# The last pass of three graph sums, in two parts: the last full chunk's tail between them, short mixes, halves

## The chip, the cores and the metric

The kernel runs on one core of one Trainium2 chip. The metric is device time in microseconds of one execution. A core has TensorE (PE, matmuls; PEld its weight loads), VectorE (DVE), ScalarE (ACT), GpSimd (POOL, which here issues the row gathers) and SyncE (SP, which issues plain DMAs).

## The reference

A graph of N = 12500 nodes with 128 features and 212500 edges, sorted by destination. Two relational layers, then one plain layer, each with a sum over the edges that end in a node:

```python
def rgcn(x, W, SW, b):                    # twice, 8 relations
    xt = einsum('nd,rde->rne', x, W)
    agg = segment_sum(xt[rel, src], dst)
    return relu(agg + x @ SW + b)
x1 = rgcn(x, w1, sl1, b1)
z  = layernorm(x + rgcn(x1, w2, sl2, b2))
feat = relu(z @ W1 + b1)                  # second part
h   = feat * d_invsqrt                    # d_invsqrt = max(degree, 1) ** -0.5
agg = segment_sum(h[src], dst)
out = layernorm(z + (feat - agg * d_invsqrt) @ W2 + b2)
```

## The kernel before

**Tiles, groups, passes.** The edges are cut into tiles of 128, seven tiles (KG) make a group, two groups a pair (PAIR), eight groups (RING) an iteration. There are 1661 tiles, thus 29 full iterations (IT) and six groups left over: five of seven tiles and one of two (`LEFT`). The kernel makes three passes over all edges: `relational_sum` twice and `plain_sum` once, each a block of its own with all engines meeting between them. Each pass gathers a 128-feature row per edge from a table in HBM: the input, then x1, then h. A pass needs the whole table of the one before it.

**A relational pass.** GpSimd (`Gathers.run`, L530) issues one indirect DMA per tile (L538) into a ring of 56 tiles. It is held by `idx_ready` alone, which ScalarE raises when it copies the indices of a pair whose ring slots have been summed. TensorE zeroes a PSUM bank (L666), in pass 1 also counts the edges per node (L675, added up by VectorE at L762), and sums a group with one matmul per tile (L681) against a one-hot matrix that VectorE made (L715, L718 for the counts, L720). It waits for all tiles of the group first (`wait_rows`, L566). ScalarE copies the bank out (L628). At the end of an iteration TensorE mixes all its groups over the eight relations (L689, eight matmuls; a float32 matmul leaves two records) and VectorE adds each group's 64 columns to the accumulator (L772). The offsets of a pair's tiles come from the table `off_i`, seven integers per group, which TensorE loads into registers.

**The plain pass.** No relations, no mix: TensorE sums a pair into one bank (L845) and VectorE adds it (L888).

**Chunks and tails.** The nodes are cut into 25 chunks (NCH) of 512, the last of 212 (two blocks of 128 where others have four). `by_chunk` (L458) is the order of every engine: for each chunk the iterations that its nodes still need, then `late`, the chunk's dense tail. In pass 1 that is the self-loop matmul's result plus the sum (L1089), activation (L1066), transposes (L971), copy (L1094) and store. Pass 2 adds a residual, a layer norm (L1392, L1396, L1194, L1403), the matmul with W1 (L1177), L1260, L1202, L1265 and three stores. In pass 3: L1338, L971, L1362, L1365, L978, L1341, L1328, L1369, a layer norm (L1373 to L1403) and the store of the output. Semaphores order the engines; each engine's own order is as written. For the last two chunks `by_chunk` runs the remaining iterations, then the six left-over groups as one iteration, then the tails of both chunks step by step together:

```python
    reach(NCH - 1)
    iteration(IT, LEFT)
    late(eng, two, [])
```

The prologue computes how many rounds a pass needs (`rounds_i`): one, unless some tile or group spans more nodes than a window has, or the left-over groups reach below the last two chunks (L360, L361).

## Time and profile before

| | us |
|---|---|
| median of 3 runs (6350.53 to 6352.94) | 6351.35 |
| the profiled execution | 6353.09 |
| its span, first to last instruction | 6351.3 |
| GpSimd busy | 4719.5 (74%) |
| TensorE busy | 3434.3 (54%) |
| VectorE busy | 1586.1 (25%) |
| ScalarE busy | 507.8 (8%) |
| mean granted TensorE clock, share of full speed | 0.645 |

Busy leaves out time in which an engine issues, waits or runs control instructions. An engine with 74% may thus be the one that never rests. The span falls into pass 1 (until about 2135), pass 2 (until 4253) and pass 3.

### The profile page before, as it was taken

What the parts mean: (1) busy time and instruction counts of PE and PEld (TensorE: products, weight loads), DVE (VectorE), ACT (ScalarE), POOL (GpSimd) and SP (SyncE); (2) the same over time, 40 slices, a digit from 0 to 9 for tenths busy, and PEclk for the clock granted to TensorE, in tenths of its full rate; (3) what the DMA queues carried; (4) which work ended last, traced back from release to release, by engine and by line L of the source; (5) the groups of instructions that cost most, each with busy time, mean ns of one, the idle gap of its engine ahead of it and who ended that gap; (6) DMA issues with size and microseconds to landing.
All of it is one profiled execution on the core that took longest, in us unless ns stands there. A gap on an engine that the chain in (4) does not pass through costs nothing. (4 is left out here: it accounts for less than half of the span.)

```text
span 6351.3 us, 51898 instructions
## 1 busy us (share of the span) xinstructions
PE 3434.3 (54%) x13350; PEld 2426.7 (38%) x13500; DVE 1586.1 (25%) x2504; ACT 507.8 (8%) x1112; POOL 4719.5 (74%) x4994
## 2 busy tenths in 40 slices
PE   4565556556565756566556656653444434344443
PEld 2333333333343534333333333333333334333333
DVE  4333433433343112122221212211111111111111
ACT  1000000000010101011110111110000000000000
POOL 6777777777777677777777777757777777777776
PEclk7776777767777767677667777765555555555555
DMA  3222222222222122222222222222222222222221
GB/s 74 59 59 59 59 56 59 59 59 59 59 59 59 52 64 74 61 69 69 69 69 61 77 61 69 69 60 58 63 61 64 62 57 68 58 62 62 62 63 55
DMA packets 207369, 396.37 MB, mean 62 GB/s; under 512 B 87746, under 2 KB 96756, under 8 KB 207332
## 3 DMA queue, kind: packets, MB, share of 16 engines
q0 software_dynamic: 159456, 326.88, 19.7%
q1 hardware_dynamic: 47876, 69.05, 3.4%
q8 instruction: 17, 0.28, 0.0%
q14 instruction: 20, 0.16, 0.0%
HBM read 363.49 MB, written 32.10 MB: 62 GB/s over the span
## 5 line engine op out<-in xcount | busy, mean ns | idle before, releaser
L538 POOL DMA_INDIRECT r_rows<-h_d,r_idx x1661 | 1568.8, 944 | 542.1 <-issue 505.9
L538 POOL DMA_INDIRECT r_rows<-x_d,r_idx x1661 | 1576.0, 949 | 531.5 <-issue 505.8
L538 POOL DMA_INDIRECT r_rows<-in_x_dram,r_idx x1661 | 1571.8, 946 | 533.7 <-issue 505.8
L681 PE MATMUL bank<-r_S,r_rows 128*128 128x128 f32 x6644 | 1218.9, 356 | 987.4 <-DMA r_rows<-in_x_dram,r_idx 455.9
L681 PEld LDWEIGHTS bank<-r_S,r_rows 128*128 128x128 f32 x6644 | 1135.5, 263 | 967.1 <-issue 957.2
L845 PE MATMUL bank<-r_S,r_rows 128*128 128x64 f32 x3322 | 768.4, 424 | 1111.2 <-DMA r_rows<-h_d,r_idx 1099.1
L845 PEld LDWEIGHTS bank<-r_S,r_rows 128*128 128x128 f32 x3322 | 726.4, 330 | 1155.7 <-DMA r_rows<-h_d,r_idx 621.2
L720 DVE TENSOR_TENSOR r_S<-bank,key 128x1792 f32<-128x1792 f32 x238 | 480.1, 2017 | 996.4 <-PE bank L681 993.7
L628 ACT COPY r_agg<-bank 128x512 f32<-128x512 f32 x476 | 279.1, 586 | 2558.2 <-PE bank L681 2558.2
L689 PE MATMUL bank<-r_agg,w1s 128*128 128x512 f32 (+1 forms) x480 | 446.7, 1099 | 24.1 <-ACT r_agg L628 24.1
L689 PE MATMUL bank<-r_agg,w2s 128*128 128x512 f32 (+1 forms) x480 | 446.3, 1098 | 24.1 <-ACT r_agg L628 24.1
L888 DVE TENSOR_TENSOR acc<-acc,bank 128x64 f32 x238 | 52.7, 222 | 1594.6 <-PE bank L845 1578.9
L715 DVE TENSOR_TENSOR r_hot<-bank,b_spot 128x1344 bf16<-128x1344 f32 x119 | 185.3, 1557 | 647.0 <-PE bank L681 641.6
L772 DVE TENSOR_TENSOR acc<-acc,bank 128x64 f32 x476 | 105.5, 222 | 794.8 <-PE bank L689 740.2
L718 DVE TENSOR_REDUCE r_part<-r_hot 128x192 bf16<-128x1344 bf16 x119 | 288.7, 2426 | 4.1
L689 PEld LDWEIGHTS bank<-r_agg,w1s 128*128 128x128 f32 x480 | 110.6, 237 | 315.1 <-issue 315.1
L689 PEld LDWEIGHTS bank<-r_agg,w2s 128*128 128x128 f32 x480 | 110.8, 237 | 314.4 <-issue 314.4
L666 PEld LDWEIGHTS bank<-zeros_bf 128*128 128x128 bf16 x476 | 53.3, 112 | 446.1 <-issue 293.3
L666 PE MATMUL bank<-zeros_bf 128*128 128x512 bf16 x327 | 152.7, 467 | 127.0 <-ACT r_agg L628 71.9
L523 ACT COPY r_idx<-src_i 128x14 int32 x360 | 73.1, 205 | 1728.0 <-PE bank L845 1728.0
L861 DVE TENSOR_TENSOR r_S<-bank,key 128x896 f32<-128x896 f32 x119 | 129.7, 1091 | 36.2 <-DVE acc L888 36.0
L675 PE MATMUL bank<-one_bf,r_part 128*32 128x1 bf16 x714 | 36.5, 166 | 156.4 <-issue 97.3
(142 smaller groups left out, 1300.8 us busy)
## 6 DMA issues: line engine op xcount, KB each, us to landing
r_rows<-in_x_dram,r_idx POOLq DMA_INDIRECT x1661, 2.5
r_rows<-x_d,r_idx POOLq DMA_INDIRECT x1661, 2.5
r_rows<-h_d,r_idx POOLq DMA_INDIRECT x1661, 2.5
d_xr<-in_x_dram SPq DMA_DIRECT2D x48, 256.0 KB, 2.7
x_d<-d_yr SPq DMA_DIRECT2D x24, 256.0 KB, 2.1
d_x1r<-x_d SPq DMA_DIRECT2D x24, 256.0 KB, 2.7
z_d<-d_zr SPq DMA_DIRECT2D x24, 256.0 KB, 2.3
feat_d<-d_fr SPq DMA_DIRECT2D x24, 256.0 KB, 2.1
```

The source lines that it names most:

```text
L523: act.copy(self.cols(p), self.c.src_i[:, bass.ds(i * UN + p * PT, PT)]).then_inc(self.idx_ready, 1)
L538: pool.indirect_dma_start(out=self.rows[:, s, :], out_offset=None, in_=self.table[:, :], in_offset=bass.IndirectOffsetOnAxis(ap=self.idx[: ...
L628: act.copy(agg[:, h, :, :], agg_ps[h % BUFS][:, :].rearrange("p (n r) -> p n r", r=NREL)).then_inc(agg_out, 1)
L666: pe.matmul(agg_ps[j][:, :], c.zeros_bf[:, :], c.zeros, start=True, stop=False, skip_group_check=True)
L681: mm = pe.matmul(agg_ps[j][:, bass.ds(offs[j * KG + k], TK)], g.rows[:, h * KG + k, :], S[:, pb, j * KG + k, :], start=False, stop=(k == t ...
L689: mm = pe.matmul(mix_ps[:, 0:groups * GN], W[:, r, :], agg[:, 0:groups, :, r], start=(r == 0), stop=(r == NREL - 1))
L715: ch.then(dve.tensor_tensor(hot[:, b, :, :], spots.unsqueeze(1).broadcast_to([P, PT, SPOTS]), bc_last(c.blocks.spot[:, at], SPOTS), ALU.is ...
L718: dve.tensor_reduce(part[:, b, :, :], hot[:, b, :, :].rearrange("p (j k) n -> p j n k", k=KG), AX.X, ALU.add)
L720: dve.tensor_tensor(S[:, b, :, :], c.iota[:, :].unsqueeze(1).broadcast_to([P, PT, TK]), bc_last(c.key[:, at], TK), ALU.is_equal).then_inc( ...
L772: ins = dve.tensor_tensor(window, window, mix_ps[:, j * GN:(j + 1) * GN], ALU.add)
L845: mm = pe.matmul(sum_ps[b][:, j * GN:(j + 1) * GN], g.rows[:, h * KG + k, :], S[:, b, j * KG + k, :], start=(k == 0), stop=(k == tiles[h] ...
L861: dve.tensor_tensor(S[:, p % BUFS, :, :], c.iota[:, 0:GN].unsqueeze(1).broadcast_to([P, PT, GN]), bc_last(c.key[:, bass.ds(i * UN + p * PT ...
```

## The change

- `by_chunk`: the six left-over groups become two parts, pair 0 (two groups) and pairs 1 and 2 (four groups). On every engine but GpSimd and SP the order is now: part one, tail of chunk 23, part two, tail of chunk 24. GpSimd's gathers keep their order.
- Within these parts TensorE mixes each pair by itself right after its sums (128 columns), and VectorE adds it right then. Full iterations mix all eight groups as before.
- The last pair (groups 4 and 5) waits for its gathers in two halves each: the first half of a group's tiles on the group's semaphore, the rest on one of two new semaphores.
- `off_i` gets 16 integers per pair in place of 14, set to zero in the prologue, and TensorE loads 16.
- The prologue's condition for a further round is tested per part. SP stores the last two chunks one after the other instead of stage by stage.

The diff, cut to its core (`...` marks what is left out):

```diff
+class Part:
+    def __init__(self, at, tiles):
+        self.at, self.tiles, self.groups = at, tiles, len(tiles)
+        self.pairs = range(at, at + len(tiles) // PAIR)
+    def of(self, h):
+        return self.tiles[h - self.at * PAIR]
+FULL = Part(0, [KG] * RING)
+LEFT = Part(0, [min(KG, TILES - g * KG) for g in range(IT * RING, NG)])
+LEFT_PARTS = [Part(0, LEFT.tiles[:PAIR]), Part(1, LEFT.tiles[PAIR:])]
+ENDS = len(LEFT.pairs)
...
+        c.off_i = sb("off_i", [1, NGP, OFFS], I32)
...
+        for at, part in enumerate(LEFT_PARTS):
+            first = IT * RING + part.at * PAIR
+            ch.then(dve.tensor_reduce(sp[:, 6 + at:7 + at], c.glo[0:1, first:first + part.groups], AX.X, ALU.min))
+            ch.then(dve.tensor_scalar(sp[:, 6 + at:7 + at], sp[:, 6 + at:7 + at], float((NCH - 2 + at) * CH), None,
+                                      ALU.is_lt))
+        ch.then(dve.tensor_tensor(sp[:, 6:7], sp[:, 6:7], sp[:, 7:8], ALU.max))
...
-    iteration(IT, LEFT)
-    late(eng, two, [])
+    for part, chunk in zip(LEFT_PARTS, two):
+        iteration(IT, part)
+        late(eng, [chunk], [])
...
+def halves(part, h):
+    tiles = part.of(h)
+    return (tiles + 1) // 2 if part is not FULL and h >= (ENDS - 1) * PAIR else tiles
...
+                    for k in range(part.of(h)):
+                        s, slot = h * KG + k, h if k < halves(part, h) else RING + h % PAIR
                         pool.indirect_dma_start(
                             out=self.rows[:, s, :], out_offset=None, in_=self.table[:, :],
                             in_offset=bass.IndirectOffsetOnAxis(ap=self.idx[:, s:s + 1], axis=0)
-                        ).then_inc(self.landed[h], 16)
+                        ).then_inc(self.landed[slot], 16)
...
+        tiles, half = part.of(h), halves(part, h)
+        if k == 0:
+            pe.wait_ge(self.landed[h], (i * KG + half) * 16)
+        elif k == half:
+            pe.wait_ge(self.landed[RING + h % PAIR], (tiles - half) * 16)
...
+                def mix(at, h0, groups):
+                    pe.wait_ge(agg_out, n + (h0 + groups + BUFS))
+                    pe.wait_ge(added, q * NIT + i + (at + 1))
+                    for r in range(NREL):
+                        mm = pe.matmul(mix_ps[:, 0:groups * GN], W[:, r, :], agg[:, h0:h0 + groups, :, r],
+                                       start=(r == 0), stop=(r == NREL - 1))
+                    mm.then_inc(mixed, 1)
...
-                        c.off_i[0:1, bass.ds(i * RING + p * PAIR, PAIR), :], engines=bass.OrderedEngineSet([pe.engine]),
+                        c.off_i[0:1, bass.ds(i * PR + p, 1), :], engines=bass.OrderedEngineSet([pe.engine]),
...
+                    if part is not FULL:
+                        mix(p, p * PAIR, PAIR)
+                if part is FULL:
+                    mix(0, 0, RING)
...
+                def add(at, starts):
+                    dve.wait_ge(mixed, q * NIT + i + (at + 2))
+                    for j, start in enumerate(starts):
+                        window = c.acc[:, bass.ds(start, GN)]
+                        ins = dve.tensor_tensor(window, window, mix_ps[:, j * GN:(j + 1) * GN], ALU.add)
+                        if j < len(starts) - 1:
+                            ch.then(ins)
+                    ins.then_inc(added, 1)
+                    dve.wait_ge(added, q * NIT + i + (at + 2))
...
+                    if ahead(part, p):
                         one_hot((p + BUFS) % PR, q, i + (p + BUFS) // PR, ch)
-                starts = load(c.gs_i, NPAD)
-                dve.wait_ge(mixed, q * NIT + i + 2)
-                for j, start in enumerate(starts):
-                    window = c.acc[:, bass.ds(start, GN)]
-                    ins = dve.tensor_tensor(window, window, mix_ps[:, j * GN:(j + 1) * GN], ALU.add)
-                    if j < len(starts) - 1:
-                        ch.then(ins)
-                ins.then_inc(added, 1)
-                dve.wait_ge(added, q * NIT + i + 2)
+                    if part is not FULL:
+                        add(p, starts[first:first + PAIR])
+                if part is FULL:
+                    add(0, load(c.gs_i, NPAD))
...
-        store(*two)
+        for ch in two:
+            store(ch)
```

## Rows read from the trace of the kernel before

**Rows 1.** costliest groups by line over the whole span; columns: line, engine, operation, tiles, shapes, count | busy us, mean ns of one | idle us before, by releaser

```profile
L538 POOL DMA_INDIRECT r_rows<-x_d,r_idx x1661 | 1576.0, 949 | 531.5 <-issue 505.8 <-ACT r_idx L517 25.7
...
L538 POOL DMA_INDIRECT r_rows<-h_d,r_idx x1661 | 1568.8, 944 | 542.1 <-issue 505.9 <-ACT r_idx L517 36.3
```

**Rows 2.** timeline, end of pass 1; columns: start us, us, engine, line, operation, tiles, count [idle before <-releaser]

```profile
2069.09 15.05 PE L689 MATMUL bank<-r_agg,w1s 128*128 128x512 f32 x16 [0.81 <-ACT r_agg L628]
...
2089.36 0.39 PE L666 MATMUL bank<-zeros_bf 128*128 128x512 bf16 x1 [1.23 <-ACT r_agg L628]
...
2094.17 2.01 DVE L720 TENSOR_TENSOR r_S<-bank,key 128x1792 f32<-128x1792 f32 x1
...
2099.86 3.35 PE L681 MATMUL bank<-r_S,r_rows 128*128 128x128 f32 x14 [5.33 <-DMA r_rows<-in_x_dram,r_idx]
...
2108.65 3.35 PE L681 MATMUL bank<-r_S,r_rows 128*128 128x128 f32 x14 [4.76 <-DMA r_rows<-in_x_dram,r_idx]
...
2114.03 11.39 PE L689 MATMUL bank<-r_agg,w1s 128*128 128x384 f32 x16 [0.75 <-ACT r_agg L628]
...
2125.56 1.98 DVE L772 TENSOR_TENSOR acc<-acc,bank 128x64 f32 x6 [21.11 <-PE bank L689]
...
2130.44 1.02 DVE L1094 COPY d_yr<-bank 128x512 f32<-128x512 f32 x2 [1.65 <-PE bank L971]
```

**Rows 3.** windows, one stretch; columns: us, PE, PEld, DVE, ACT, POOL busy, granted clock, DMA share

```profile
2091.00:2099.00 8.00, 3.35 (x14) 3.09 (x15) 5.35 (x5) 0.59 (x1) 6.16 (x7) 0.50 0.22 55
```

**Rows 4.** timeline, a tail inside the loop of pass 2

```profile
4124.43 0.69 DVE L1240 TENSOR_TENSOR d_pre<-bank,acc 128x512 f32<-128x512 f32 x1 [0.56 <-DVE acc L772]
...
4133.07 2.08 PE L1177 MATMUL bank<-gw1s,d_zT 128*128 128x128 f32 x8 [0.68 <-ACT d_zT L1198]
...
4136.67 0.69 DVE L1265 TENSOR_TENSOR d_hr<-d_fr,dinv 128x512 f32<-128x512 f32 x1 [0.79 <-ACT d_fr L1202]
...
4142.26 3.26 PE L681 MATMUL bank<-r_S,r_rows 128*128 128x128 f32 x14 [4.18 <-issue]
...
4148.73 1.82 PE L681 MATMUL bank<-r_S,r_rows 128*128 128x128 f32 x14
```

**Rows 5.** timeline, end of pass 2

```profile
4194.99 0.59 ACT L628 COPY r_agg<-bank 128x512 f32<-128x512 f32 x1 [1.19 <-PE bank L681]
...
4221.40 11.28 PE L689 MATMUL bank<-r_agg,w2s 128*128 128x384 f32 x16 [0.75 <-ACT r_agg L628]
...
4232.82 1.99 DVE L772 TENSOR_TENSOR acc<-acc,bank 128x64 f32 x6 [34.32 <-PE bank L689]
...
4248.11 1.03 DVE L1265 TENSOR_TENSOR d_hr<-d_fr,dinv 128x512 f32<-128x512 f32 x2
```

**Rows 6.** groups by line and shape, the two-block chunk's instructions

```profile
L1066 ACT ACTIVATE d_xT<-d_xT,b1s 128x256 f32<-128x256 f32 x1 | 0.5, 493 | 0.0
...
L1362 DVE TENSOR_TENSOR d_ag<-bank,dinv 128x256 f32<-128x256 f32 x1 | 0.4, 417 | 0.0
```

**Rows 7.** timeline of pass 3: a tail inside its loop, then its end

```profile
6216.72 0.57 DVE L888 TENSOR_TENSOR acc<-acc,bank 128x64 f32 x2 [15.53 <-PE bank L845]
...
6223.39 2.08 PE L1328 MATMUL bank<-gw2s,d_uT 128*128 128x128 f32 x8 [0.67 <-ACT d_uT L1341]
...
6228.99 1.11 DVE L1403 TENSOR_SCALAR d_o<-d_r,d_mv,d_rstd 128x128 f32<-128x128 f32 x4
...
6304.00 0.58 DVE L888 TENSOR_TENSOR acc<-acc,bank 128x64 f32 x2 [15.16 <-PE bank L845]
...
6326.80 0.94 POOL L538 DMA_INDIRECT r_rows<-h_d,r_idx  x1 [0.30 <-issue]
...
6326.88 4.38 PE L845 MATMUL bank<-r_S,r_rows 128*128 128x64 f32 x18 [5.55 <-DMA r_rows<-h_d,r_idx]
...
6331.39 0.57 DVE L888 TENSOR_TENSOR acc<-acc,bank 128x64 f32 x2 [9.35 <-PE bank L845]
...
6346.12 0.75 DVE L1403 TENSOR_SCALAR d_o<-d_r,d_mv,d_rstd 128x128 f32<-128x128 f32 x2
```

More of the change, by code:

```diff
@@ L34 @@
 TILES = -(-E // P)
[L35 to L36 removed]
+class Part:
[8 more added lines that the diff above has]
+ENDS = len(LEFT.pairs)
 NGP = NG // PAIR
[L38 to L39 removed]
+OFFS = 16
+assert NT % KG == 0 and min(LEFT.tiles) > 0 and NG % PAIR == 0 and RING % PAIR == 0 and PR % BUFS == 0
+assert LEFT.groups % PAIR == 0 and BUFS < ENDS < PR and PAIR == BUFS and PT <= OFFS
 CH = 512
@@ L203, in __init__ @@
         self.raw_in = [sem(f"raw_in{n}") for n in range(3)]
-    CONSTS = 11
+    CONSTS = 12
     BANKS = -(-NTB // 4)
@@ L530, in run, with iteration @@
     def run(self, pool, ready):
-        def iteration(q, i, tiles):
-            for p in range(len(tiles) // PAIR):
+        def iteration(q, i, part):
+            for p in part.pairs:
                 pool.wait_ge(self.idx_ready, (q * (IT + 1) + i) * PR + p + 1)
@@ L590, in relational_sum @@
     hot = sb("hot", [P, BUFS, PT, SPOTS], BF16) if counts else None
-    part = sb("part", [P, BUFS, PAIR, SPOTS], BF16) if counts else None
+    placed = sb("placed", [P, BUFS, PAIR, SPOTS], BF16) if counts else None
     hot_ready = sem("hot_ready")
@@ L621, in _, with iteration @@
         with act.Fori(0, rounds) as q:
-            def iteration(i, tiles):
+            def iteration(i, part):
                 n = act.snap(q * NG + i * RING)
@@ L625, in iteration @@
                 gate(act, c.passed)
-                for h in range(len(tiles)):
+                for h in range(part.at * PAIR, part.at * PAIR + part.groups):
                     act.wait_ge(summed, n + (h + 1 + RING))
@@ L629, in iteration @@
                              ).then_inc(agg_out, 1)
-                    if tiles is FULL and h % PAIR == PAIR - 1:
+                    if part is FULL and h % PAIR == PAIR - 1:
                         g.take(act, h // PAIR, q, i + 1)
@@ L724, in _, with ahead, part_steps @@
         first_steps = BUFS if counts else 0
-        def pass_steps(tiles):
-            pairs = len(tiles) // PAIR
-            ahead = pairs if tiles is FULL else max(pairs - BUFS, 0)
-            return (pairs + ahead if counts else 0) + len(tiles) - 1
-        round_steps = first_steps + IT * pass_steps(FULL) + pass_steps(LEFT)
+        def ahead(part, p):
+            return part is FULL or p + BUFS < ENDS
+        def part_steps(part):
+            adds = part.groups - 1 if part is FULL else len(part.pairs) * (PAIR - 1)
+            return (len(part.pairs) + sum(ahead(part, p) for p in part.pairs) if counts else 0) + adds
+        left_steps = [part_steps(part) for part in LEFT_PARTS]
+        round_steps = first_steps + IT * part_steps(FULL) + sum(left_steps)
         with dve.Fori(0, rounds) as q:
@@ L742, in _, with iteration @@
             gate(dve, c.passed)
-            def iteration(i, tiles):
-                n = dve.snap(q * NG + i * RING)
+            def iteration(i, part):
                 np = dve.snap(q * NGP + i * PR)
-                pairs = len(tiles) // PAIR
-                ch = Chain(dve, steps, q * round_steps + (i * pass_steps(FULL) + first_steps))
+                before = left_steps[0] if part is LEFT_PARTS[1] else 0
+                ch = Chain(dve, steps, q * round_steps + (i * part_steps(FULL) + (first_steps + before)))
                 def load(table, most):
                     _, values = nc.values_load_multi_w_load_instructions(
-                        table[0:1, bass.ds(i * RING, len(tiles))], engines=bass.OrderedEngineSet([dve.engine]),
+                        table[0:1, bass.ds(i * RING + part.at * PAIR, part.groups)],
+                        engines=bass.OrderedEngineSet([dve.engine]),
                         min_val=0, max_val=most, skip_runtime_bounds_check_because="clamped on the chip")
                     return values
+                def add(at, starts):
[7 more added lines that the diff above has]
+                    dve.wait_ge(added, q * NIT + i + (at + 2))
                 blocks_at = load(c.blocks.gb_i, DEG_COLS) if counts else None
-                for p in range(pairs):
+                starts = load(c.gs_i, NPAD) if part is not FULL else None
+                for p in part.pairs:
+                    first = (p - part.at) * PAIR
                     if counts:
@@ L814, in _, with iteration @@
         with act.Fori(0, rounds) as q:
-            def iteration(i, tiles):
-                if tiles is FULL:
+            def iteration(i, part):
+                if part is FULL:
                     for p in range(PR):
@@ L833, in _, with iteration @@
             gate(pe, c.passed)
-            def iteration(i, tiles):
+            def iteration(i, part):
                 np = pe.snap(q * NGP + i * PR)
-                for p in range(len(tiles) // PAIR):
+                for p in part.pairs:
                     b = p % BUFS
```

74 lines of the change are left out of this document (31 added, 43 removed).

## The prediction

> **What bounds the kernel now.** I first read the groups by line. GpSimd issues 1661 row gathers in each of three passes: 944 to 949 ns of work each and 0.30 us of issue idle, so one starts every 1.25 us [rows 1]. Its only other long idle time is at a seam: 25.7 us before pass 2's first gather, 36.3 us before pass 3's. Three passes at 1.25 us are 6.23 ms of the 6.35 ms span, so inside a pass TensorE, VectorE and ScalarE are covered. What the change can move is the stretch from the last gather of a pass to the next first gather, and from the last gather of all (start 6326.80) to the end [rows 7].
>
> The timelines show what fills them. In pass 1 the last sums are followed by one mix over six groups (384 columns) that starts at 2114.03 and takes 11.39 us, six adds that end at 2127.54, and the tails of chunks 23 and 24 together, whose last copy ends at 2131.46 [rows 2]. Pass 2 has the same from 4221.40, adds until 4234.81, and a longer tail until 4249.14 [rows 5]. Pass 3 has no mix: the last adds end at 6331.96, the tail at 6346.87 [rows 7], the span at 6351.3.
>
> **What the change does, part by part.**
>
> *Price of a short mix.* Sixteen records at 512 columns take 15.05 us, at 384 columns 11.39, so 128 columns are worth 3.66 us and a mix of one pair (128 columns) costs 11.39 - 7.32 = 4.1 us [rows 2]. The first add starts 11.5 us after the start of the long mix, so 4.2 after a short one. The Trainium skill, "Perfetto Trace Analysis", Matmuls, says that larger matmuls are more efficient than smaller ones when possible, which speaks against three mixes for one. By that rule the three would cost more than the 11.39 us. The rows give 12.3 against 11.4, nearly straight in the columns, so I add 0.9 us in all, most of it off the end.
>
> *TensorE, pass 1.* Pair 0 is summed before 2089. Its mix is over by 2093, but VectorE makes the one-hots for pair 2 first, until 2096.2 [rows 2]. Then two adds (0.6), the tail of chunk 23: first add 0.7, activation 0.7, four transposes 1.1, gaps: TensorE is free at about 2099.8. It used to sum group 2 long before and group 3 at 2099.86. Now it loads its offsets (a gap of 1.23 us before the zeroing matmul at 2089.36 [rows 2]) and counts: group 2 starts at 2101.3. A group takes 3.35 us with granted clock 0.50, the 1.2 GHz level [rows 2, 3], and 1.82 us at the higher level, 2.4 GHz; in pass 2 sums go from 3.26 to 1.82 us once TensorE has stayed at work [rows 4]. I take 3.35 for group 2, 2.6 for group 3 and 1.8 for group 4. Group 2 ends at 2104.7, group 3 at 2107.5, the mix of pair 1 runs 2108.3 to 2112.2 (0.8 us for the last copy, as before 2114.03). Group 4's rows had landed at 2108.65 [rows 2], group 5's two, two gathers later, at 2111.2: neither is waited for, so halves are worth nothing here. Group 4 ends at 2114.4, group 5 at 2115.2, mix 2116.0, adds 2120.2 to 2120.8. Before: 2127.54. Gain 6.7 us.
>
> *Tail of the short chunk alone, pass 1.* Before: 3.92 us from adds to last copy. Now 0.23 + add 0.42, activation 0.49 [rows 6], two transposes 0.6 (four 0.26 us records, by the rate of the eight in 2.08 [rows 4]), copy 0.42, gaps 0.15: 2.3. Gain 1.6. Pass 1 together 8.3.
>
> *Pass 2.* Pair 0's last copy is at 4194.99, so its mix starts at 4195.8, the adds at 4199.9 (VectorE makes one one-hot only and is not late), chunk 23's first instruction at 4200.7. In the loop the tail keeps TensorE until the end of L1177, 4124.43 to 4135.15: 10.7 us [rows 4]. So TensorE is free at 4211.4 and group 2 starts at 4212.9 (offsets, zeroing), ends 4216.2; group 3 4219.1; mix 4219.9 to 4223.8; group 4 4225.8; group 5 4226.6; mix 4227.4; adds 4231.5 to 4232.1, against 4234.81: gain 2.7. The tail took 14.33 us for both chunks [rows 5]. One chunk of four blocks takes 12.93 in the loop (4124.43 to 4137.36 [rows 4]). With two blocks: four VectorE passes save 0.27 each (0.69 to 0.42), three of ScalarE 0.23 each (0.72 to 0.49) [rows 4, 6], two sets of transposes 0.5 each and the matmuls 1.0, the per-block instructions (scaling 1.11 us for four [rows 7], statistics about as much) half, 1.05. Together 4.8: 8.1, with the first gap 8.3. Gain 6.0. Pass 2 together 8.7.
>
> *Pass 3.* Pair 0's adds end at 6304.6; the tail in the loop holds TensorE from the adds at 6216.72 to the end of L1328 at 6225.47, 8.8 us, and VectorE to 6230.10, 13.4 us [rows 7]. So TensorE is back at about 6312.8, before group 3's rows, and VectorE at 6317.4, before pair 1's adds (6321): all of chunk 23 is hidden under gathers. Group 4's first four tiles are summed while the other three come; from 6326.88 three tiles take 1.4 us and not 3.25. The last row set lands 2.57 us after its gather starts (group 4's last gather is two before 6326.80 and its sum starts 6326.88): 6329.37, one tile 0.65: adds at 6330.15 and not 6331.39 [rows 7]. Gain 1.2. The tail was 14.9 us; in the loop one of four blocks is 12.8 from the end of the adds (6217.29 to 6230.10 [rows 7]); less 0.5 for a later start there and 4.6 for two blocks: 7.7. Gain 7.2. Pass 3 together 8.4.
>
> *What I cost at nothing.* The 16 loaded offsets for 14 lie on TensorE, covered by gathers; at the two ends between -0.5 and +0.5 us each, taken 0 (no row separates a load). The wider memset of the offsets and three small VectorE instructions, by rows 6 (1.07 ns per column) about 2 + 0.6 us, lie before the first sums while GpSimd runs ahead by up to eight groups; uncovered they would cost 2.6. The stores in chunk order instead of stage order move SP's issues only; both chunks' stores are now apart, 0 to -0.5. The 4.4 us after the last instruction stay. The gather queue has the same 1661 gathers, two semaphores more. New waits: VectorE's adds for pair p stand ahead of the next pair's counts and TensorE's mix ahead of the next pair's sums; both are in the times above.
>
> Sum: 8.3 + 8.7 + 8.4 = 25.4. From the profiled execution's own 6353.09 us that is 6327.7; the median of the runs is 1.74 lower, so 6326.
>
> **Rivals.**
>
> *The catching-up stays at 1.2 GHz.* The tail in the middle puts waits between TensorE's bursts. After such waits in the loop of pass 2 it started again at 3.26 us per group [rows 4], and the waiting stretch of pass 1 had clock 0.50 [rows 3]. Groups 3, 4 and 5 then cost 0.75, 1.5 and 0.5 more in passes 1 and 2: 5.5 us less gain, 19.9, time 6331.5. Against: pairs 1 and 2 have all rows there, and TensorE waits only for one copy at a time. The Trainium skill, "TensorE: Matmul & The Clock Gate", Why this matters for your kernels, warns of long idle gaps between matmul bursts because they drop the clock; this trace agrees (3.26 us per group behind the gap, 1.82 later). By that rule the new gaps make this rival's time.
>
> *A dear restart.* Behind a tail in the loop TensorE idled 4.18 us in issue [rows 4]. The new seam is straight code, not a jump back, but if it costs the same, passes 1 and 2 lose 3 us each: 19.4 of gain, 6332; with the low clock 13.9, 6337.5.
>
> *The time is saved nowhere* (the common seam, a barrier or a DMA receipt, sets the next start): passes 1 and 2 would give nothing and only pass 3's 8.4 stay, 6343. Against: the next first gather follows the last copy within 4 us, with nothing else under way.
>
> *Slower: gathers themselves.* GpSimd's mean is 949 ns in pass 2 and 944 in pass 3 for the same instruction [rows 1], so its pace depends on neighbours. If the moved tables and other addresses cost 10 ns per gather, 4983 of them take 50 us, and the kernel would need 6376. It decides from 5.1 ns per gather on. Against: its loop, its reads and its 0.30 us issue are untouched.
>
> *The change doesn't hold its condition:* if part two's groups reached below node 12288 another round would run, over 2 ms. By the data it doesn't: part two starts with edge 209,664 of 212,500, and nodes from 12288 on have about 212 x 17 = 3600 edges, so it begins some 45 nodes above.
>
> **Numbers.** Forecast (gain 23 to 30) 0.55, low clock 0.22, dear restart 0.11, nothing at the seams 0.05, slower gathers 0.05, the rest 0.02. Best case: the high clock at once takes 2.3 us more from each of passes 1 and 2, 6321.4. Range 6319 to 6338. What a measurement can tell from no change is 0.2%, 12.7 us. Faster 0.91, same 0.05, slower 0.04.
>
> **What would show it.** Right: GpSimd's idle before pass 2 near 17.4 us and before pass 3 near 27.6; 16-record mixes of 128 columns near 4.1 us; last adds of pass 3 about 3.4 us after the last gather's start and 8 us of tail. Group 4's sum at 1.8 us tells the forecast from the low clock; the gap between the middle tail's last matmul and group 2 tells of the restart. Wrong: mean gather above 950 ns, or the last adds of passes 1 and 2 not earlier than before.

## The result, and the profile after

| | median us | range, runs | ratio to before |
|---|---|---|---|
| kernel before | 6351.44 | 6350.53 to 6352.94, 6 | |
| changed kernel | 6321.93 | 6320.77 to 6327.29, 6 | 0.9955, 95% 0.9942 to 0.9967 |

The forecast was 6326; the change brought 29.5 us where 25.4 were worked out. The profiled execution of the changed kernel was its longest, 6327.29 us with a span of 6325.5, so against the span of 6351.3 before it shows 25.8 us. I cut both spans at the gathers: "seam" is from the start of a pass's last gather to the start of the next pass's first, "end" from the last gather of all to the last instruction.

| us | start to first gather | pass 1 | seam 1 | pass 2 | seam 2 | pass 3 | end |
|---|---|---|---|---|---|---|---|
| before | 31.80 | 2076.69 | 26.60 | 2080.81 | 37.24 | 2073.66 | 24.50 |
| after | 34.48 | 2077.75 | 16.03 | 2079.89 | 24.87 | 2075.30 | 17.18 |
| difference | +2.68 | +1.06 | -10.57 | -0.92 | -12.37 | +1.64 | -7.32 |

The seams and the end gave 30.3 us. The start took 2.7 back. The passes themselves scatter by a few us: in a second profile of the changed kernel (a0_after below) pass 2 was 2073.9 and everything else within 1.3 us of this table.

The groups of GpSimd's gathers in the profile after, columns as in [rows 1]:

```profile
L570 POOL DMA_INDIRECT r_rows<-x_d,r_idx x1661 | 1575.1, 948 | 520.8 <-issue 505.7 <-ACT r_idx L548 15.1
L570 POOL DMA_INDIRECT r_rows<-in_x_dram,r_idx x1661 | 1573.0, 947 | 536.3 <-issue 505.7 <-ACT r_idx L548 30.6
L570 POOL DMA_INDIRECT r_rows<-h_d,r_idx x1661 | 1570.6, 946 | 529.6 <-issue 505.7 <-ACT r_idx L548 23.9
```

The pace of the gathers is as in [rows 1], 946 to 948 ns. The idle time ahead of pass 2 fell from 25.7 to 15.1 us, ahead of pass 3 from 36.3 to 23.9. At the start it rose, from 27.9 to 30.6.

The timeline of pass 1's end, which answers to [rows 2] (PE is TensorE, DVE VectorE, POOL GpSimd):

```profile
2092.53 3.96 PE L699 MATMUL bank<-r_agg,w1s 128*128 128x128 f32 x16 [0.75 <-ACT r_agg L664]
...
2100.26 0.56 DVE L808 TENSOR_TENSOR acc<-acc,bank 128x64 f32 x2
...
2102.55 1.13 PE L1028 MATMUL bank<-ident,d_xT 128*128 128x128 f32 x4 [6.06 <-ACT d_xT L1123]
...
2103.81 0.60 PE L711 MATMUL bank<-zeros_bf 128*128 128x512 bf16 x1
...
2104.59 3.35 PE L727 MATMUL bank<-r_S,r_rows 128*128 128x128 f32 x14
...
2108.07 1.73 PE L727 MATMUL bank<-r_S,r_rows 128*128 128x128 f32 x14
...
2112.23 0.94 POOL L570 DMA_INDIRECT r_rows<-in_x_dram,r_idx  x1 [0.30 <-issue]
...
2114.89 1.83 PE L727 MATMUL bank<-r_S,r_rows 128*128 128x128 f32 x14
...
2118.13 3.96 PE L699 MATMUL bank<-r_agg,w1s 128*128 128x128 f32 x16 [0.75 <-ACT r_agg L664]
...
2122.22 0.57 DVE L808 TENSOR_TENSOR acc<-acc,bank 128x64 f32 x2 [6.36 <-PE bank L699]
...
2124.58 0.42 DVE L1151 COPY d_yr<-bank 128x256 f32<-128x256 f32 x1 [1.14 <-PE bank L1028]
...
2128.26 0.94 POOL L570 DMA_INDIRECT r_rows<-x_d,r_idx  x1 [15.09 <-ACT r_idx L548]
```

Pair 0's mix and the whole tail of chunk 23 (up to the transposes, 2103.68) lie before the last gather starts at 2112.23. Behind it stand what is left of pair 1, the sums and the mix of pair 2, two adds and a two-block tail. The adds end 10.56 us after the last gather's start, before 19.05.

Granted clock in windows over this stretch, columns as in [rows 3]:

```profile
2100.00:2112.00 12.00, 8.57 (x46) 7.33 (x47) 2.37 (x7) 1.89 (x3) 9.18 (x10) 0.67 0.28 77
2112.00:2125.00 13.00, 9.84 (x55) 7.99 (x53) 2.02 (x8) 2.30 (x7) 0.94 (x1) 1.00 0.06 12
```

After the wait for chunk 23's tail TensorE runs one group at 1.2 GHz (3.35 us); the next already takes 1.73, and from 2112 on the granted clock is 1.00, 2.4 GHz.

The end of pass 2, which answers to [rows 5]:

```profile
4201.44 2.08 PE L1234 MATMUL bank<-gw1s,d_zT 128*128 128x128 f32 x8 [0.68 <-ACT d_zT L1255]
4203.31 0.63 PE L711 MATMUL bank<-zeros_bf 128*128 128x512 bf16 x1
...
4203.73 3.19 PE L727 MATMUL bank<-r_S,r_rows 128*128 128x128 f32 x14
...
4207.15 1.74 PE L727 MATMUL bank<-r_S,r_rows 128*128 128x128 f32 x14
...
4216.80 3.97 PE L699 MATMUL bank<-r_agg,w2s 128*128 128x128 f32 x16 [0.75 <-ACT r_agg L664]
...
4220.90 0.57 DVE L808 TENSOR_TENSOR acc<-acc,bank 128x64 f32 x2 [6.57 <-PE bank L699]
...
4229.29 0.43 DVE L1322 TENSOR_TENSOR d_hr<-d_fr,dinv 128x256 f32<-128x256 f32 x1 [0.48 <-ACT d_fr L1259]
```

The last gather started at 4208.15; the adds end 13.32 us later (before 18.91), the tail 8.25 us after them (before 14.33). The way from the last copy to the next pass's first gather is shorter too: 3.26 against 3.63 us behind pass 1, 3.30 against 4.00 behind pass 2.

The end of pass 3, which answers to [rows 7]:

```profile
6304.64 1.94 PE L901 MATMUL bank<-r_S,r_rows 128*128 128x64 f32 x8 [1.67 <-DMA r_rows<-h_d,r_idx]
...
6308.27 1.98 PE L901 MATMUL bank<-r_S,r_rows 128*128 128x64 f32 x8 [1.68 <-DMA r_rows<-h_d,r_idx]
6308.32 0.94 POOL L570 DMA_INDIRECT r_rows<-h_d,r_idx  x1 [0.30 <-issue]
6311.70 0.69 PE L901 MATMUL bank<-r_S,r_rows 128*128 128x64 f32 x2 [1.45 <-DMA r_rows<-h_d,r_idx]
6312.52 0.57 DVE L944 TENSOR_TENSOR acc<-acc,bank 128x64 f32 x2 [8.82 <-PE bank L901]
...
6320.36 0.60 DVE L1460 TENSOR_SCALAR d_o<-d_r,d_mv,d_rstd 128x128 f32<-128x128 f32 x2
```

The last tile's sum starts 3.38 us after its gather, not 2.57, and it still ends on a DMA wait. The two waits ahead of it ended 2.56 and 2.44 us after the start of the gather that they needed, so 2.57 holds for gathers ahead of the last.

### The profile page after: what moved, and what is told of

It reads as the page before. It is cut to its first block and busy times, and to the rows that moved or that the text cites. A ratio compares the mean times of both kernels' runs of the same rounds, so it can differ in the third digit from the quotient of the medians.

```text
span 6325.5 us, 52193 instructions
## 1 busy us (share of the span) xinstructions
PE 3487.7 (55%) x13563; PEld 2458.0 (39%) x13564; DVE 1588.9 (25%) x2508; ACT 508.5 (8%) x1112; POOL 4721.7 (75%) x4994
## 5 line engine op out<-in xcount | busy, mean ns | idle before, releaser
L727 PE MATMUL bank<-r_S,r_rows 128*128 128x128 f32 x6644 | 1246.6, 362 | 1043.4 <-DMA r_rows<-x_d,r_idx 527.2
L727 PEld LDWEIGHTS bank<-r_S,r_rows 128*128 128x128 f32 x6644 | 1169.0, 269 | 1166.8 <-issue 1155.1
L901 PEld LDWEIGHTS bank<-r_S,r_rows 128*128 128x128 f32 x3322 | 726.6, 330 | 1145.9 <-DMA r_rows<-h_d,r_idx 621.5
L761 DVE TENSOR_REDUCE r_placed<-r_hot 128x192 bf16<-128x1344 bf16 x119 | 289.1, 2430 | 4.1
L711 PE MATMUL bank<-zeros_bf 128*128 128x512 bf16 x476 | 232.8, 489 | 82.1 <-issue 82.0
L1028 PE MATMUL bank<-ident,d_xT 128*128 128x128 f32 x98 | 27.6, 434 | 120.4 <-ACT d_xT L1123 120.4
```

What stands on the lines that cost most here:

```text
L711: pe.matmul(agg_ps[j][:, :], c.zeros_bf[:, :], c.zeros, start=True, stop=False, skip_group_check=True)
L727: mm = pe.matmul(agg_ps[j][:, bass.ds(offs[j * KG + k], TK)], g.rows[:, h * KG + k, :], S[:, pb, j * KG + k, :], start=False, stop=(k == t ...
L761: dve.tensor_reduce(placed[:, b, :, :], hot[:, b, :, :].rearrange("p (j k) n -> p j n k", k=KG), AX.X, ALU.add)
L901: mm = pe.matmul(sum_ps[b][:, j * GN:(j + 1) * GN], g.rows[:, h * KG + k, :], S[:, b, j * KG + k, :], start=(k == 0), stop=(k == tiles - 1))
```

## The experiments

Twelve kernels ran, the changed kernel itself among them, on four chips. On two of them the kernel before took 6350 and 6349 us. On the third it took 8041 and on the fourth, which ran only the last experiment, 8023: there GpSimd waits for free ring slots for hundreds of microseconds, so times from these two are read only as ratios to the kernel before on the same chip. It is not the rows that come late. The median gather's last packet ends 2.19 us after the gather's start on the third chip (e8) as in the changed kernel's first profile. It is TensorE. At the end of e8's pass 3 its weight loads start 2.8 us apart, with nothing shown that they wait for:

```profile
7947.91 0.95 POOL L571 DMA_INDIRECT r_rows<-h_d,r_idx  x1 [0.30 <-issue]
7948.02 0.28 PEld L902 LDWEIGHTS bank<-r_S,r_rows 128*128 128x128 f32 x1 [2.52 <-issue]
7949.42 0.27 PE L902 MATMUL bank<-r_S,r_rows 128*128 128x64 f32 x1 [2.53 <-issue]
7950.82 0.28 PEld L902 LDWEIGHTS bank<-r_S,r_rows 128*128 128x128 f32 x1 [2.52 <-issue]
```

The first line is the last gather; its last packet ends 3.13 us after its start, but its tile is summed only at 7976.4, 28 us after it. Weight loads 2.8 us apart (2.75 to 2.85) come 108 to 138 times in each of the five traces from these two chips, and never in the changed kernel's first profile. What slows TensorE there is not shown.

### What each part is worth

The changed kernel again (a0_after), beside three that undo one part each.

> The changed kernel again, on the chip of the other runs. Its first profile came from its slowest execution (6327.29 us, first gather at 34.5 us), the other five lay at 6320.8 to 6322.4. If the 2.7 us at the start come from the change (the wide memset of the offset table stands ahead of the loads), the first gather is at 34.5 us here too. If they are chance of one execution, it is near 31.8, and the median stays at 6322.

Measured: 6321.12 (6319.59 to 6322.51, 5 runs) against 6349.92 of the kernel before on the same chip, ratio 0.9956 (0.9943 to 0.9970). First gather at 34.37 us, seams 16.56 and 24.70, end 17.15. The result repeats, the late start too.

**e1_tails_together**: short mixes, halves and offsets stay, but chunk 23's tail goes back behind part two.

```diff
         iteration(IT, part)
-        late(eng, [chunk], [])
+    late(eng, two, [])
```

> The tails of both last chunks stand together at the end again; mixes by pair and halves stay. Theory (the tail in the middle is worth its length, hidden under gathers): pass 1 about +1 us against the changed kernel (its tail is short, and TensorE is free earlier), pass 2 +3, pass 3 +7, in all 6333, so 18 of the 29.5 us remain. Rival (the short mixes carry the gain, the middle tail only moves work and delays TensorE): within 3 us of the changed kernel, 6322 to 6325.

Measured: 6332.68 (6331.10 to 6336.54, 10 runs), 0.9975 (0.9966 to 0.9985) of before; 11.6 above a0_after on its chip. By stretch against a0_after: seam 1 +0.26, seam 2 +3.61, end +7.3, close to the theory's 1, 3 and 7. The middle tail is worth 11.6 of the 28.8 us there, nearly all in passes 2 and 3, whose tails are long. In pass 1 the middle tail is worth next to nothing: with it the adds end 1.73 us later, for pair 1's sums wait for chunk 23, and what follows them is 2.0 us shorter. In pass 2 it costs the adds 3.6 us and saves 7.2 behind them. The end of this kernel's timeline shows what the other chunk costs on VectorE after the last adds:

```profile
6310.15 0.57 DVE L944 TENSOR_TENSOR acc<-acc,bank 128x64 f32 x2 [8.84 <-PE bank L901]
...
6323.84 1.11 DVE L1460 TENSOR_SCALAR d_o<-d_r,d_mv,d_rstd 128x128 f32<-128x128 f32 x4 [0.40 <-DVE d_rstd L1436]
...
6325.30 0.60 DVE L1460 TENSOR_SCALAR d_o<-d_r,d_mv,d_rstd 128x128 f32<-128x128 f32 x2
```

15.2 us from adds to the last instruction, against 7.87 in the changed kernel.

**e2_one_mix**: part two mixes pairs 1 and 2 together, 256 columns at once.

```diff
-                    if part is not FULL:
-                        mix(p, p * PAIR, PAIR)
+                if part is not FULL:
+                    mix(part.at, part.at * PAIR, part.groups)
```

> Pairs 1 and 2 are mixed together at the end (256 columns) and added then; tail in the middle and halves stay. Theory (a mix costs in proportion to its columns, 3.7 us per 128, and only what stands behind the last gather counts): pass 1 +3.7 us against the changed kernel, pass 2 +0.9 since TensorE is busy there from the middle tail on, pass 3 nothing, in all 6326.5. Rival (larger matmuls are cheaper, three starts cost more than they save): not slower than the changed kernel, 6322 or below.

Measured: 6328.35 (6325.60 to 6329.12, 6 runs), 0.9966 (0.9954 to 0.9978); 7.2 above a0_after. Seam 1 is 3.29 longer, seam 2 1.11. The timeline of TensorE at the end of its pass 1:

```profile
2116.09 0.53 PE L727 MATMUL bank<-r_S,r_rows 128*128 128x128 f32 x2 [1.93 <-DMA r_rows<-in_x_dram,r_idx]
2117.36 7.74 PE L699 MATMUL bank<-r_agg,w1s 128*128 128x256 f32 x16 [0.75 <-ACT r_agg L664]
```

All of the 7.74 us starts after the last rows are summed. With short mixes pair 1's 3.96 us are done by then: in the changed kernel that mix runs from 2110.55, around the last gather's start. The other 2.8 us of the median are not explained; the profiles' passes and starts scatter by as much.

**e3_no_halves**: a group waits for all its rows.

```diff
-    return (tiles + 1) // 2 if part is not FULL and h >= (ENDS - 1) * PAIR else tiles
+    return tiles
```

> Each group of the last pair waits for all its tiles at once; the rest stays. My prediction gave the halves 1.2 us, all in pass 3. The trace after shows that the last gather lands 3.4 us after its start and not 2.6, so the sum of group 4 is over by then either way. Theory now: 0.4 us, two tiles instead of one behind the last landing, 6322.3. By the prediction's sizes: 1.2 us, 6323.2.

Measured: 6322.72 (6320.30 to 6324.20, 5 runs), 0.9959 (0.9945 to 0.9972). The medians differ by 1.6 with ranges that overlap, so they can't tell 0.4 from 1.2; the trace can. The end is 0.52 longer, seam 1 0.08 and seam 2 0.88 shorter. The halves gain half a microsecond at the end, not 1.2.

### The offsets and the late start

The gain was larger than forecast and the start later. Both had to do with the edit of the offsets' table that I had costed at nothing.

**e4_offsets14** takes the table back: 14 integers per pair, rows of 56 bytes, no zeroing of the table.

```diff
-        c.off_i = sb("off_i", [1, NGP, OFFS], I32)
+        c.off_i = sb("off_i", [1, NG, KG], I32)
...
-                        c.off_i[0:1, bass.ds(i * PR + p, 1), :], engines=...
+                        c.off_i[0:1, bass.ds(i * RING + p * PAIR, PAIR), :], engines=...
```

> The offset table is as before the change: 14 integers per pair, not padded, not set to zero in the prologue, TensorE loads 14. The rest is the changed kernel. The first gather starts at 34.1 to 35.0 us in all five profiles of changed kernels and at 31.8 before. Theory (the table's edit causes it): first gather back at 31.8 and a median 2.7 us below the changed kernel, 6318.5. Rival (it is another part, such as the longer program): first gather at 34.4, median 6321. By my prediction (the table costs nothing) also 6321.

**e8_memset_late** keeps 16 and moves their zeroing behind the computation of the tables.

```diff
-        for ap, value in ((c.zeros_bf[:, :], 0.0), (c.one_bf[:, :], 1.0), (c.off_i[:, :, :], 0), (c.eps[:, :], EPS),
+        for ap, value in ((c.zeros_bf[:, :], 0.0), (c.one_bf[:, :], 1.0), (c.eps[:, :], EPS),
...
+        ch.then(dve.memset(c.off_i[:, :, :], 0))
         node_blocks(dve, c, ch, c.glo)
```

> The table stays padded, but is set to zero only after the first gathers have started (in VectorE's chain ahead of the node blocks). If the memset at 2 to 3.6 us delays the loads, the first gather is back at 31.8 and the median at 6318.5. If it is the table's size (all tiles allocated behind it lie 952 bytes further in SBUF, the tile that the loads write among them), it stays at 34.4 and the median at 6321. The SyncE issues are longer in the changed kernels even at 18 us (5.1 us against 4.8), when the memset is long over, which speaks for the second.

Both ran on the third chip, where the kernel before took 8040.92 (7998.68 to 8076.70). e4: 8053.17 (8032.83 to 8080.50, 12 runs), ratio 1.0017 (0.9996 to 1.0038). e8: 7992.79 (7976 to 8007, 12 runs), 0.9947 (0.9931 to 0.9962). First gather at 32.61 in e4, at 34.71 in e8: the zeroing is not what delays the start, something that comes with the new table is. And between the two lie 0.7%, 60 us. Two things change with the table: how the offsets are loaded, and where everything behind it lies. In the kernel before the accumulator begins on a multiple of 64 bytes, in the changed one 32 bytes off; the gathered rows of passes 1, 2 and 3 go from 32, 0, 0 bytes past a multiple of 64 to 0, 32, 32.

The loads have rows of their own in every profile, the kernel before's among them. Columns: line, the sequencer of TensorE, operation, count; duration in ns, least/median/most. The kernel before, the changed kernel, e10 (below) and e17 (below):

```profile
L660 PEldq TENSOR_LOAD <-off_i x238: 1338/3309/3372, 71.5 to 4208.0; - x119
L705 PEldq TENSOR_LOAD <-off_i x238: 1100/1107/1123, 72.7 to 4209.7; - x119
L704 PEldq TENSOR_LOAD <-off_i x238: 1338/3344/3693, 77.8 to 4210.0; - x119
L703 PEldq TENSOR_LOAD <-off_i x238: 700/3311/3686, 74.0 to 5526.0; - x119
```

A load of 14 integers takes 3.3 us in the median, a load of 16 takes 1.11 us, wherever accumulator and rows lie. In the kernel before the loads of a pass's even pairs mostly take 2.7 us (94 of 116 in the full iterations of both passes), those of its odd pairs 3.35 (all 116). The table begins on a multiple of 64 bytes. In it an even pair's 56 bytes begin on a multiple of 16, an odd pair's 8 bytes past one; every eighth pair begins on a multiple of 64, and its load takes 2.7 us or more too. So a start on a multiple of 64 does not by itself make a load of 14 cheap. The left-over pairs take 1.35, 3.33 and 1.34 us: the one load that the change moves to the seam, pair 1's, is a dear one.

**e10_shift32** is e4 with 32 unused bytes ahead, so that the accumulator lies as in the changed kernel; **e14_aligned64** is the changed kernel with accumulator and rows on multiples of 64.

```diff
+        c.pad = sb("pad", [1, 8], I32)                      # e10, on e4
         c.gs_i = sb("gs_i", [1, NG], I32)
...
-        c.acc = sb("acc", [P, ACC])                          # e14, on the changed kernel
+        c.acc = sb("acc", [P, ACC], align_bytes=64)
...
-nc.sbuf_tensor(f"{tag}_rows", [P, UN, D], F32)
+nc.sbuf_tensor(f"{tag}_rows", [P, UN, D], F32, align_bytes=64)
```

> The offset table of before (14 integers, no memset) and behind it 32 spare bytes, so that all tiles behind it start 32 bytes further: the accumulator, into which the prologue loads the edges, at 32 and no longer at 0 modulo 64, as in the changed kernel; the rest is the changed kernel. With the table of before and no spare bytes the first gather started at 32.6 us, with the wide table set to zero late at 34.7. Theory (place, not the table's content or its memset, delays the loads): SyncE's long issues take 5.1 us or more and the first gather starts at 34.4. Rival (width or number of loaded offsets): 32.6 or less.

> The changed kernel with the accumulator and all three gather rings placed on multiples of 64 bytes (in the changed kernel the accumulator and the rings of passes 2 and 3 lie at 32 modulo 64, before it only the ring of pass 1 did). Theory: loads as fast as before, first gather at 31.8 to 32.6, so 2.5 us below the changed kernel: 6318.5 where that takes 6321. On a chip where a gather's landing is the bound (as that of the last four runs, with 8041 us before) the rings' place decides more: passes 2 and 3 shorter than in the changed kernel too, below 7990. Rival (place of the accumulator doesn't matter): first gather at 34.4.

Measured on one chip (before: 6349.07, 6346.66 to 6353.48): e10 6327.95 (6326.16 to 6329.40, 6 runs), 0.9966 (0.9954 to 0.9979); e14 6321.01 (6319.36 to 6321.96, 5 runs), 0.9956 (0.9943 to 0.9970). The 6.9 us between them are the first gather (37.30 against 35.70), seam 1 (18.58 against 15.44) and seam 2 (26.13 against 24.07). My figure for e14's start, 31.8 to 32.6, was a miss: on this chip every first gather came late. The 1.6 us between the two are not firm either: e15 (below), placed like e14, had its first gather at 36.99. My figure for slow chips (below 7990) was not tried, for e14 ran on none; its premise, that a gather's landing is the bound there, does not hold (see above). Timeline of TensorE behind the middle tail's transposes in pass 1, e10:

```profile
2103.95 1.13 PE L1027 MATMUL bank<-ident,d_xT 128*128 128x128 f32 x4 [6.14 <-ACT d_xT L1122]
2107.80 0.60 PE L710 MATMUL bank<-zeros_bf 128*128 128x512 bf16 x1 [2.72 <-issue]
```

the same place in e14:

```profile
2102.25 1.13 PE L1028 MATMUL bank<-ident,d_xT 128*128 128x128 f32 x4 [6.06 <-ACT d_xT L1123]
2103.51 0.61 PE L711 MATMUL bank<-zeros_bf 128*128 128x512 bf16 x1
```

Only the register load of the offsets stands between these two lines. It starts together with the transposes, and the zeroing starts 0.15 us after its end. In e10 it takes 3.70 us, so TensorE sits idle for 2.72; in e14 it takes 1.10 and hides behind the transposes but for 0.13. In pass 2 the same gap is 1.44 us in e10 and nothing in e14. The two gaps, 4.0 us, are most of the 5.2 by which e10's seams are longer. Over all pairs of both passes TensorE's idle time ahead of the zeroing matmuls is 366.6 us in e10 and 82.1 in the changed kernel. Inside a pass the gathers hide it; at a seam nothing does.

**e17_offsets14_aligned64** has both: 14 offsets as in e4, accumulator and rows on multiples of 64 as in e14. It is to tell the loads from the placement.

> The changed kernel with its offsets as before, 14 loaded per pair from wherever they begin (a row of 28 bytes), and with the accumulator and the gathered rows on multiples of 64 bytes; against e14_aligned64 it differs in the offsets alone. Theory: the loads of 16 aligned offsets close the gap ahead of a pair's zeroing matmul. Then the gap between the middle tail's last transpose and the zeroing matmul of pass 1 is 1.2 us or more here, against 0.1; the stretch from the last gather of pass 1 to the first of pass 2 is about 18.5 us (15.4 in e14), that of pass 2 about 26 (24.1), and the median is 6326, 5 above e14's 6321. Rival: the 7 us between e10_shift32 and e14_aligned64 come from where the rows and the accumulator lie; then this kernel has e14's seams and 6321. The start tells of the placement alone: by its theory the first gather comes as in e14 or earlier, 35.7 us or less, where e10 had 37.3.

It came to the fourth chip, as slow as the third, so 6326 could not be read there. Measured: 8036.56 (8007.73 to 8073.61, 12 runs) against 8023.05 (7997.16 to 8061.72), ratio 1.0017 (0.9999 to 1.0035): that of e4 on the third chip to the fourth digit, with the other placement, where all three kernels with 16 offsets have 0.9947 or 0.9948 on the third chip. It is a comparison of ratios across two slow chips: no kernel with 16 offsets ran on the fourth. At the same place in pass 1 TensorE is idle for 3.24 us in e17 and for 0.66 in e8, 16 offsets on the third chip (the zeroing's record is missing in both, so each gap holds its half microsecond too), and the loads there take 3.68 and 1.10 us. The gap goes with the loads and not with the placement.

For the 0.7% that is not shown. By the profiles the gain is not where the loads alone would put it:

| us | pass 1 | pass 2 | seam 2 | pass 3 |
|---|---|---|---|---|
| e4: 14 offsets, third chip | 2662 | 2787 | 58.5 | 2440 |
| e17: 14 offsets, fourth chip | 2618 | 2787 | 58.6 | 2432 |
| e8: 16 offsets, third chip | 2539 | 2819 | 73.1 | 2434 |

With 16 offsets pass 1 is 78 to 123 us shorter, but pass 2 and its seam are 47 us longer together (47 to 52 in e5 and e6, below). Where the rows of pass 2 lie changes too (on a multiple of 64 in e4 and e17, 32 bytes past it in e8, e5 and e6). These runs don't separate the two.

The start goes with the placement on these chips: first gather at 32.25 in e17 and, on the third chip, 32.61 in e4 (accumulator on a multiple of 64), but 34.69 to 34.75 in the three kernels with 16 offsets there (accumulator 32 bytes off). There it goes with the table as well; only e10 and e14, on a chip of 6349 us, cross the two. SyncE's issues of the first loads show where. The changed kernel:

```profile
2.05 4.03 SPq L231 DMA_DIRECT2D acc<-in_dst_dram  x1
9.57 5.23 SPq L231 DMA_DIRECT2D acc<-in_src_dram  x1
18.20 5.07 SPq L231 DMA_DIRECT2D acc<-in_edge_type_dram  x1
```

the kernel before:

```profile
2.06 3.67 SPq L215 DMA_DIRECT2D acc<-in_dst_dram  x1
8.69 4.83 SPq L215 DMA_DIRECT2D acc<-in_src_dram  x1
16.75 4.83 SPq L215 DMA_DIRECT2D acc<-in_edge_type_dram  x1
```

e17's are 3.77, 4.75 and 4.83 us. The edges are staged through the accumulator's memory. With the accumulator 32 bytes off, two of the three issues take over 5 us; on the multiple of 64, 4.83 at most. On the chip of e10 and e14 the two are 5.67 and 5.67 in e10 (14 offsets, 32 bytes off), 5.44 and 5.33 in e14, 5.42 and 5.34 in e15 (16 offsets, on the multiple): slower for all, in the order of the placement and against that of the table. So the placement has a part in the late start; that it makes all of the 2.7 us is not shown, and neither is why.

### The last gather's rows

Three kernels asked why the last tile comes 3.4 us after its gather and whether more can be had at the seam.

**e5_extra_gather** lets GpSimd issue one more gather behind the last, of rows that nothing sums. If a gather's rows are pushed out by the next gather, the needed tile lands sooner.

```diff
             iteration(q, IT, LEFT)
+            s = LEFT.groups * KG - 1
+            pool.indirect_dma_start(out=self.rows[:, s, :], ..., in_=self.table[:, :], ...).then_inc(self.spare, 16)
```

> One more gather (1.25 us of GpSimd, into a ring slot that nobody reads) behind the last one of every pass; all else is the changed kernel. The sum of the last tile waits 3.4 us from the start of the last gather, while a group's last gather inside the stream is there 2.45 to 2.57 us after its start. Theory (a gather's landing is seen earlier when another one follows): in pass 3 the last needed tile is summed 0.8 us earlier, 2.5 us after its gather's start, end 16.3 instead of 17.2; passes 1 and 2 nothing, for TensorE is late there by itself. Rival (the last one just lands so late, or the follower adds its own time): 3.4 or 4.6 us. The median moves by under 1 us either way; the trace decides.

**e6_add_first** lets VectorE add pair 0 before it makes the one-hots of pair 2, so that chunk 23's tail starts some 4 us sooner.

```diff
+                if part is LEFT_PARTS[1]:
+                    one_hot(BUFS, q, i, ch)
                 for p in part.pairs:
...
-                    if ahead(part, p):
+                    if part is FULL:
```

> VectorE adds pair 0 before it makes the one-hots of pair 2; these come after the middle tail. In the trace after, pass 1's pair 0 was mixed at 2096.5 but added only at 2100.26, behind the one-hots. Theory: in pass 1 the middle tail and all TensorE work behind it start 3.6 us earlier, until the last pair's landing becomes the bound: the last mix starts 1.3 us earlier; pass 2 (one one-hot, no counts) and 3 the same. Seam 1 15.0 instead of 16.3, median 6320. Rival (TensorE's catching up isn't the bound of pass 1): no change of seam 1.

Both ran on the third chip: 7997.32 (0.9948, 0.9931 to 0.9966) and 7994.81 (0.9948, 0.9931 to 0.9965), level with e8's 7992.79. There TensorE sums so late (the last adds of pass 3 end 30.6 and 29.2 us after the last gather's start) that neither question is answered. So both edits went, with e14's placement, into one kernel, **e15_aligned_first_extra**, beside e14:

> The aligned kernel, and with it VectorE's adds of pair 0 ahead of the one-hots of pair 2, and one spare gather behind the last of each pass. Theory: first gather 32; seam 1 (last needed gather to first of pass 2) 15.0 instead of 16.3 since the last mix starts 1.3 us earlier; the end 16.3 instead of 17.2, since the last needed tile is summed 2.5 us after its gather's start instead of 3.4; in all 6316.5. Rival (TensorE's catching up isn't the bound of pass 1, and the last landing is late by itself): the same as the aligned kernel, 6318.5.

Measured: 6319.59 (6317.91 to 6323.94, 5 runs), 0.9953 (0.9939 to 0.9967); 1.4 under e14, with ranges that overlap: no difference that these runs can tell. In pass 3 the last needed tile is summed 3.40 us after its gather's start, against 3.38 in the changed kernel and 3.72 in e14: a gather behind it changes nothing.

The traces hold a rival that no run tests. In every pass of the changed kernel the last gather itself is the slow one: its 32 packets take 0.22 to 0.25 us on average and the last ends 3.0 to 3.1 us after the gather's start; the gather ahead of it has 0.12 to 0.15 and 2.1 to 2.25. The last tile holds the last 20 edges, and its other 108 indices are padding, all 0, so it reads one row 108 times. Whether that makes it slow could be told by padding with different rows.

The adds first bring the middle tail forward, and TensorE in its pass 1 shows why that gains so little (seam 1 is 15.01 against 15.44 in e14, where 1.3 us were expected):

```profile
2108.69 3.97 PE L706 MATMUL bank<-r_agg,w1s 128*128 128x128 f32 x16 [0.75 <-ACT r_agg L670]
...
2117.29 0.48 PE L734 MATMUL bank<-r_S,r_rows 128*128 128x128 f32 x2 [1.63 <-DMA r_rows<-in_x_dram,r_idx]
2118.53 3.97 PE L706 MATMUL bank<-r_agg,w1s 128*128 128x128 f32 x16 [0.75 <-ACT r_agg L670]
```

TensorE now waits 1.63 us for the last rows. The last needed gather started at 2113.84, so the last mix starts 4.69 us after it, against 5.11 in e14. What stands behind the last gather is then its landing, the sum, one copy, the mix, two adds and the short tail.

## Why the prediction was right, and where its sizes were off

The mechanism held: GpSimd's pace bounds the passes, and the gain lies at the two seams and the end alone. That the sum came within some 4 us is in part luck: the seams gave 6.0 us more than worked out, the start and the end 3.8 less. By its steps:

- *Short mix, 4.1 us.* 3.96 and 3.97. Nearly straight in the columns (256 take 7.74 in e2). Three short mixes take 11.9 us where the long one took 11.39, so larger ones are cheaper, by 0.5 us in all; I had added 0.9.
- *Tails of the short chunk: 2.3, 8.3 and 7.7 us.* 2.21, 8.25 and 7.87. Scaling by blocks from rows of the four-block chunk was enough.
- *Chunk 23's tail under gathers.* Right: e1, which takes it back, loses 11.6 us, though next to nothing of it in pass 1.
- *TensorE free before the last gather.* Forecast 8.7 us (pass 1) and 4.5 us (pass 2) before its start; measured 8.55 and 4.63.
- *Restart, 1.5 us in each of passes 1 and 2 from TensorE free to group 2's sum, 1.2 of them the offsets: mis-sized, and for the wrong reason.* Measured 0.91 and 0.21; the gap ahead of the zeroing is 0.13 and nothing (4203.31 is before the modelled end of the matmul ahead of it). I read the 1.23 us of [rows 2] as what TensorE needs to load offsets, though the row says that they ended on ScalarE's copy. I costed the new layout of these offsets, the one edit that touches the load, at -0.5 to +0.5, with the remark that no row separates a load. One does: the kernel before's own profile has 3.31 us in the median and 3.33 for this pair. With the old layout the gap at the new place is 2.72 us in pass 1 and 1.44 in pass 2 (e10), so the edit was worth about 4 us at the two seams. The rival of a dear restart rested on the same load: of its 4.18 us [rows 4] 2.75 are the load (4138.89 to 4141.64 in that profile). At the same place of the changed kernel the idle time is 2.13. Without the new layout that rival would have been half true.
- *Low clock.* The profile decided against that rival: 3.35 and 3.19 us for the first group, then 1.73 and 1.74. I had 2.6 for the second, between the levels, so 0.9 us more in each pass.
- *Halves, 1.2 us.* Worth 0.4 to 0.5 (from the last gather's start to the last add's end 5.16 us before, 4.77 after; e3 0.52). The term that failed is the landing: I took 2.57 us from a gather ahead of the last, and the last one takes 3.4. The same step's "a tile 0.65" held (0.69 for two records).
- *Memset and start, 0 with 2.6 as the uncovered price.* The start cost 2.7, but not by the memset (e8). Where the accumulator came to lie has a part in it (e10 against e14), which I had not looked at.
- *Stores in chunk order, 0 to -0.5.* The way from the last copy to the next first gather is 0.37 and 0.70 us shorter; no run takes this edit back.

Put together: seam 1 gave 10.6 where 8.3 stood, seam 2 12.4 where 8.7 stood, the end 7.3 where 8.4 stood, the start -2.7 where 0 stood. 27.6 us; the other 1.9 up to the medians' 29.5 are within the scatter of the passes from one profile to the next.

The Trainium skill, "Runtime: NRT & Kernel Launch", Instruction fetch mechanics, gives some 200 ns per register for register loads from HBM. By that figure 14 registers would take 2.8 us and 16 would take 3.2, an estimate. Here they come from SBUF, and the trace agrees for the old table alone: 2.7 and 3.35 us for 14 are 0.19 to 0.24 us each. The 16 of the new table take 1.11 us, 0.07 each, where the measurement decides.

Open: whether a load of 16 integers is also cheap from a row that begins elsewhere (only that a start on a multiple of 64 is not enough for 14 is shown); how much of the late start the placement makes, and why; what slows TensorE on two of the chips, and why e4 and e17 gain nothing there.

## What to carry to other kernels

Where a pass is bound by a steady stream and the next pass needs all of it, move whatever does not need the last items ahead of them, and cut the batch behind the last item small: here 30 us at three such places, while TensorE's 55% and VectorE's 25% did not matter. Cost every edit at the seam, the layout of a table of register operands too. Where an idle gap in front of an instruction is put down to "issue", look for the rows of the engine's sequencer, here TENSOR_LOAD: what they take counts in full where no stream hides it. When tensors ahead of others change size, look where the others come to lie.

## What the runs showed of the hardware

- A load of 14 integers from 56-byte rows in SBUF into TensorE's registers takes 3.3 us in the median (2.7 or 3.35, by where the row begins), one of 16 from 64-byte rows 1.11 us (238 loads in each trace). At a place that nothing hides, the first leaves 2.72 and 1.44 us of idle time, the second 0.13 and nothing.
- On the third chip SyncE's issues of the second and third load took 4.74 and 4.83 us with their destination on a multiple of 64 bytes (e4; e17 on the fourth 4.75 and 4.83) and 5.40 and 5.07 at 32 bytes past it (e8). On a chip where the table's width went the other way they took 5.44 and 5.33 (e14) and 5.67 and 5.67 (e10).
- The last gather's rows were there 3.4 us after its start, whether or not another gather followed (3.38 and 3.40), those of gathers ahead of it after 2.44 to 2.56.
- TensorE's clock was back at the higher level, 2.4 GHz, after one group of 3.35 us at the lower one: the next took 1.73, and from 2112 on the granted clock was 1.00.
- Two chips of four ran the kernel before in 8041 and 8023 us. GpSimd's gathers took as long there as elsewhere (943 to 951 ns) and their rows landed as soon, but TensorE's weight loads often came 2.8 us apart with nothing shown to wait for.
